# Attention round 0: stacks fetched in the projection stage, ten maxima units beside it, round 1's units inside round 0

## The chip, the cores and the metric

The kernel runs on one core of a Trainium2 chip. The metric is the device time of one execution in microseconds: the median over several runs. One more execution is recorded by the hardware profiler; all durations below are read from it.

## The reference

Two transformer layers over 4 sequences of 1024 tokens with 256 channels, all in fp32. Layer 0 has a random-feature attention (with rotary embedding) and a mixture of 8 experts, top 2. Layer 1, around which the change lies, has causal softmax attention with 16 heads of 16 channels, and a mixture of 16 experts, top 4, with a shared expert:

```python
def _L1_attn_ref(X, Wq, bq, Wk, bk, Wv, bv, Wo, bo):
    scale = 1.0 / sqrt(sqrt(d_head))
    Q = (X @ Wq.T + bq).reshape(B, S, H, d_head) * scale
    K = (X @ Wk.T + bk).reshape(B, S, H, d_head) * scale
    V = (X @ Wv.T + bv).reshape(B, S, H, d_head)
    scores = einsum('bhqd,bhkd->bhqk', Q, K)
    scores = where(causal, scores, -inf)
    out = einsum('bhqk,bkhd->bqhd', softmax(scores), V).reshape(B, S, D)
    return out @ Wo.T + bo
```

Each layer adds attention output times silu(mixture output) to its input; a layer norm stands before each.

## The kernel before

The program is a row of phases with a barrier of all engines between them: the first attention, experts of layer 0, the projection stage of layer 1 (`gate_and_project`), the causal attention, experts of layer 1, the shared expert and the gate. Each engine (TensorE or PE, VectorE or DVE, ScalarE or ACT, GpSimd or POOL, SyncE or SP with its DMA queue) has its own program, executed in the order in which it is written; semaphores join them. There is no planner: order is written out by hand with a helper `steps`, which for n = 0, 1, ... calls each stage with its own lag, stage(n - lag).

**First attention.** POOL's `rotate` (L701) multiplies q and k by cosine and sine into rot_a and rot_b, each with two buffers, and adds them.

**Projection stage** (L1132). 32 tiles of 128 tokens. Per step POOL gathers two expert rows per token (`rows`, lag 0) and multiplies (`product`, lag 2); ScalarE and VectorE combine, gate and add the residual. With lag 8 VectorE normalises a tile and TensorE transposes it (L1294); ScalarE keeps it and its high half; VectorE takes the low half (`low_half`, lag 9, L1222). With lag 9 TensorE computes V and router logits in three fp32r passes, with lag 13 one of four query/key tiles of a chunk of 512 tokens (`features`, six matmuls of 512 columns into one of four PSUM banks psK). ScalarE takes the high half of that (lag 13), VectorE the low half (lag 14, L1237), and SyncE stores both (256 KB each, L1338), beside V (L1329), the residual (L1319) and the transposed tile. The buffers of stored query/key and V tiles are four deep. The last features come in step 44, the last store in step 45. The order in which VectorE does its stages in a step n is: inverse root (n-5), normalise (n-8), low half (n-9), combine (n-1), V (n-10), residual (n-3), query/key low half (n-14). After the last step SyncE fetches the stacks of attention round 0 with `load_stacks` (L1602: four DMAs of 512 KB, L1607 and L1609), without waiting for them to land, and waits for all stores.

**Causal attention** (L1612). 16 rounds; round n does 4 heads of one sequence. A round works on a slot of three: the query stack QS and the key stack KS (high and low halves stacked on 126 partitions), two more rows for the negative row maxima (QS) and for ones (KS), and the values VA. Before the scores of a round the row maxima of all queries are needed. They are found in 38 units (`unit`): a unit is one to four matmuls into one PSUM bank psM of three (L1903) and one reduction by VectorE, with the causal mask added (L1799, on the diagonal) or plain (L1803). The units are in order of the query tile qt: unit 0 has four heads of 128 keys, units 1 and 2 two heads of 256, units 3 to 6 one head of 384, units 7 to 10 one head of 512, and so on. `whole` joins the maxima, TensorE turns them (L1913), VectorE's `negate` makes m_hi and m_lo (L1818 to L1822), and SyncE's `maxima_rows` stores them, waits, and loads them as two rows of QS.

The round itself has 12 steps of four score tiles (TensorE, L1920), each followed by ScalarE's exponential (L1883), POOL's cut on the diagonal (L1776), and with a lag of two steps the values (TensorE, L1932). Between the score tiles of round n TensorE does units: in steps 0 to 6 units 16 to 37 of round n+1, in steps 7 to 11 units 0 to 15 of round n+2 (`ahead`). VectorE does its share of them in the same order, with one piece of the router's work in each step (`route`).

The front of the phase, before round 0: VectorE does the first ten pieces of routing (L275 to L298), then the 38 units of round 0, `whole`, `negate`, and units 0 to 15 of round 1. TensorE waits for slot 0's stacks and VA, does the units of round 0, waits for slot 1, does units 0 to 15 of round 1, and begins with the scores. SyncE loads VA 0, ones, the stacks of round 1 (after POOL has zeroed slot 1), ones, and then does `maxima_rows(0, 0)`; the stacks of round n+2 are pulled at the start of round n. POOL zeroes QS and KS of slots 1 and 2 and makes the mask (`masks`, L2095).

## Time and profile before

| | us |
|---|---|
| median of 3 runs | 1855.63 (1853.65 to 1856.06) |
| the profiled execution | 1856.16 |
| its span, first to last instruction | 1854.4 |
| busy: PE, DVE, ACT, POOL | 1612.0, 1370.4, 1033.8, 672.0 |
| mean granted TensorE clock | 0.938 of full |
| projection stage | 555 to 716 |
| causal attention | 716 to 1278 |

A row of a timeline gives the start in us from the span's start, the duration, engine and line, the instruction with the tiles it writes and reads, and, in brackets, idle time of the engine before it and what ended it. A row of the windows gives busy us (and number of instructions) of PE, PE's weight loads, DVE, ACT and POOL in a stretch, then the granted TensorE clock (1.00 is 2.4 GHz, 0.50 is 1.2 GHz), the share in which the DMA engines were busy, and GB/s. Of operations that follow without a gap, the pace is the distance of their starts; the durations of matmuls overlap.

### The profile page before, as it was taken

How to read it: one execution, taken by the hardware profiler on the slowest of the kernel's cores; microseconds unless marked ns; L12 is line 12 of the kernel's file. 1: busy time of each engine (PE TensorE's matmuls, PEld its weight loads, DVE VectorE, ACT ScalarE, POOL GpSimd, SP SyncE). 2: the span in 40 equal slices, each digit the busy share in tenths (PEclk: the TensorE clock that was granted, in tenths of full speed). 3: DMA queues.
4: the chain of work that ended last, by engine and by line, in shares of the span. 5: the costliest groups of instructions: out<-in, count | busy, mean ns of one | idle time of the engine just before them, and what ended most of it. 6: DMA issues, size and time to landing. Idle time of an engine off the chain costs nothing. (4 is left out here: it accounts for less than half of the span.)

```text
span 1854.4 us, 34559 instructions
## 1 busy us (share of the span) xinstructions
PE 1612.0 (87%) x9650; PEld 1249.2 (67%) x9650; DVE 1370.4 (74%) x3710; ACT 1033.8 (56%) x2457; POOL 672.0 (36%) x842
## 2 busy tenths in 40 slices
PE   6897787679982776999999999997899999988997
PEld 5786676569982564555455555543799999967775
DVE  6778999356667876999888888852676666657777
ACT  2554565246654762466667676765556666643443
POOL 2545588510007643021136767630000000056662
PEclk9898899889995996799999999998999999989999
DMA  9322357654434888243244645404874444355552
GB/s 344 123 69 68 94 130 187 169 166 132 133 112 133 277 294 243 55 100 76 61 118 133 172 141 168 145 29 135 262 228 133 133 132 133 119 159 168 166 166 77
DMA packets 279591, 272.72 MB, mean 147 GB/s; under 512 B 121769, under 2 KB 248426, under 8 KB 277356
## 3 DMA queue, kind: packets, MB, share of 16 engines
q1 hardware_dynamic: 255672, 215.41, 39.6%
q0 software_dynamic: 18432, 50.36, 8.9%
q10 hardware_dynamic: 5332, 4.96, 0.8%
q8 instruction: 88, 1.44, 0.3%
q14 instruction: 67, 0.55, 0.1%
HBM read 136.84 MB, written 133.69 MB: 146 GB/s over the span
## 5 line engine op out<-in xcount | busy, mean ns | idle before, releaser
L1883 ACT ACTIVATE ca_PT<-ca_psS 128x512 f32<-128x512 f32 (+3 forms) x768 | 336.4, 494 | 204.0 <-PE ca_psS L1920 199.2
L1423 POOL DMA_INDIRECT g_y<-ys_scratch,pos x128 | 125.0, 977 | 425.7 <-POOLq L73 354.2
L1799 DVE CUSTOM_DVE_ANT_0 ca_masked_row<-ca_psM,mask_row 128x384 f32<-128x384 f32 (+3 forms) x512 | 224.2, 486 | 45.0 <-PE ca_psM L1903 42.9
L1803 DVE TENSOR_REDUCE ca_part<-ca_psM 128x1 f32<-128x512 f32 x256 | 163.5, 684 | 16.8 <-PE ca_psM L1903 15.4
L1920 PE MATMUL ca_psS<-ca_QS,ca_KS 128*128 128x512 f32 (+1 forms) x480 | 174.6, 367 | 1.4 <-ACT ca_PT L1883 1.4
L1932 PE MATMUL ca_psO<-ca_PT,ca_VA 128*17 128x512 f32 (+3 forms) x1536 | 161.0, 491 | 6.0 <-ACT ca_OT L1875 6.0
L1903 PE MATMUL ca_psM<-ca_KS,ca_QS 126*128 126x512 f32 (+2 forms) x480 | 159.5, 380 | 6.5 <-DVE ca_part L1799 4.2
L790 PE MATMUL fa_psO<-fa_weighed,ident 128*128 128x256 f32 x512 | 131.8, 416 | 38.1 <-DVE fa_weighed L585 38.1
L1920 PEld LDWEIGHTS ca_psS<-ca_QS,ca_KS 128*128 128x128 f32 x480 | 90.2, 189 | 86.8 <-ACT ca_PT L1883 58.1
L790 PEld LDWEIGHTS fa_psO<-fa_weighed,ident 128*128 128x128 f32 x512 | 104.6, 210 | 60.0 <-DVE fa_weighed L585 44.4
L391 POOL DMA_INDIRECT xs_scratch<-x_sb,pos x128 | 124.6, 973 | 55.9 <-ACT ca_PT L1883 34.1
L997 PE MATMUL f_psU<-ffn_lo,f_x_hi 128*128 x428 | 139.0, 325 | 0.0
L1086 DVE TENSOR_TENSOR f_x_lo<-f_psT,f_x_hi 128x256 fp32r<-128x256 f32 x214 | 90.7, 424 | 45.8 <-ACT f_x_hi L1038 45.6
L1044 ACT ACTIVATE f_silu<-f_psU 128x176 f32<-128x176 f32 x214 | 68.1, 318 | 100.1 <-PE f_psU L997 100.1
L1018 PE MATMUL f_psY<-ffn_lo,f_h_hi 128*128 x428 | 120.1, 281 | 0.0
L1774 POOL TENSOR_TENSOR ca_waited<-ca_waited 1x1 f32<-1x1 f32 x128 | 25.6, 200 | 259.9 <-ACT ca_PT L1883 258.6
L1903 PE MATMUL ca_psM<-spare 126*128 126x512 f32 (+3 forms) x288 | 98.3, 405 | 17.1 <-DMA ca_VA<-v_scratch 16.3
L1903 PEld LDWEIGHTS ca_psM<-ca_KS,ca_QS 126*128 126x128 f32 x480 | 88.8, 196 | 36.0 <-DVE ca_part L1799 17.4
L1094 DVE TENSOR_TENSOR f_h<-f_silu,f_psU 128x96 f32<-128x96 f32 x214 | 54.3, 254 | 76.7 <-ACT f_silu L1044 76.3
L1920 PE MATMUL ca_psS<-spare 128*128 128x512 f32 (+3 forms) x288 | 104.1, 375 | 2.7 <-ACT ca_PT L1883 2.5
L997 PE MATMUL f_psU<-ffn_hi,f_x_hi 128*128 x286 | 104.6, 366 | 0.0
L391 POOL DMA_INDIRECT xs_scratch<-s,pos x64 | 84.3, 1317 | 38.9 <-PE f_psT L967 24.2
(271 smaller groups left out, 4649.5 us busy)
## 6 DMA issues: line engine op xcount, KB each, us to landing
xs_scratch<-fa_blank SPq DMA_DIRECT2D x32, 640.0 KB, 4.9
x_sb<-xs_scratch SPq DMA_DIRECT2D x143, 128.0 KB, 2.1
ys_scratch<-x_sb SPq DMA_DIRECT2D x143, 128.0 KB, 1.7
xs_scratch<-fa_blank SPq DMA_DIRECT2D x32, 384.0 KB, 6.7
spare<-qk_scratch SPq DMA_DIRECT2D x24, 512.0 KB
ca_QS<-qk_scratch SPq DMA_DIRECT2D x20, 512.0 KB, 6.2
ca_KS<-qk_scratch SPq DMA_DIRECT2D x20, 512.0 KB, 7.5
x_sb<-in_ffn SPq DMA_DIRECT2D x16, 608.0 KB, 4.1
```

Source lines behind the costliest of these rows:

```text
L391: pool.indirect_dma_start(xs_dram, bass.IndirectOffsetOnAxis(pos[:, t, k:k + 1], 0), rows[:, t, :], None).then_inc(sent[i], 16)
L790: ins = pe.matmul(psO[i % 2][:, 0:NQ], ident[:], weighed[:, i % 2, g, :], start=g == 0, stop=g == KV_HEADS - 1)
L997: ins = pe.matmul(psU[i % 2][:, 0:WU], x[:, i % 2, k * P:(k + 1) * P], w[:, bass.ds(e, 1), k * WU:(k + 1) * WU].rearrange("p a n -> p (a n)"),
L1018: ins = pe.matmul(psY[i % 2][:, 0:HID], x, w[:, bass.ds(e, 1), first:first + HID].rearrange("p a n -> p (a n)"), start=start, stop=first = ...
L1086: dve.tensor_tensor(x_lo[:, i % 2, :], psT[i % 2][:, 0:HID], x_hi[:, i % 2, :].bitcast(F32), ALU.subtract)\
L1423: pool.indirect_dma_start(y[:, t % R, k, :], None, y_dram, bass.IndirectOffsetOnAxis(pos[:, t, k:k + 1], 0)).then_inc(got[t % R], 16)
L1799: ins = dve.tensor_tensor_reduce(masked_row[:, (n * NU + u) % BANKS, h * w:(h + 1) * w], bank[:, h * w:(h + 1) * w], mask_row[:, CHUNK - w ...
L1803: dve.tensor_reduce(part[:, k0 // CHUNK, h0:h0 + nh, qt], bank[:, 0:nh * w].rearrange("p (h k) -> p h k", h=nh), AX.X, ALU.max).then_inc(u ...
L1883: act.activation(PT[:, s % PTS, h, off:CHUNK], psS[(GH * s + h) % BANKS][:, off:CHUNK], ACT.Exp)\
L1903: ins = pe.matmul(bank[:, h * w:(h + 1) * w], QS[slot][0:STACK, h0 + h, qt * P:(qt + 1) * P], KS[slot][0:STACK, h0 + h, k0:k0 + w], start= ...
L1920: pe.matmul(psS[tile % BANKS][:, off:CHUNK], KS[slot][:, h, kt * P:(kt + 1) * P], QS[slot][:, h, c * CHUNK + off:(c + 1) * CHUNK], start=T ...
L1932: ins = pe.matmul(psO[STRIP * h:STRIP * h + VW, off:CHUNK], VA[:, slot, kt, VW * h:VW * (h + 1)], PT[:, s % PTS, h, off:CHUNK], start=kt = ...
```

## The change

It has six parts.

1. In the first attention rot_a and rot_b have one buffer each; POOL waits for its own add of the tile before (`rot_done`) before it overwrites them.
2. In the projection stage psK has three banks instead of four, and the bank that is freed, psM, takes maxima units. The mask is made by POOL at the start of this stage, ahead of the gathers, and lies, with the maxima `part`, in memory that the attention keeps.
3. SyncE fetches the stacks of round 0 at the end of step 32 of this stage, between the stores.
4. Units 0 to 9 of round 0 are done in steps 36 to 45, one at the end of each step, by TensorE and by VectorE.
5. In the attention VectorE begins with units 10 to 37 of round 0, `whole` and `negate`; the first ten pieces of routing come behind them. VA 0 and the pull of round 1's stacks come behind `maxima_rows(0, 0)` on SyncE. KS of slot 1 is zeroed by ScalarE, QS of slot 1 by POOL.
6. All 38 units of round 1 are done within round 0, in steps 2 to 6 (7 or 8 in each), followed as before by units 0 to 15 of round 2 in steps 7 to 11. TensorE waits for slot 1's stacks at the start of step 2. The later rounds keep their order.

```diff
@@ -702,7 +703,9 @@
...
-                q3, a3, b3 = (x[:, i % 2, :].rearrange("p (h d) -> p h d", d=D) for x in (qk, rot_a, rot_b))
+                if t >= 1:
+                    pool.wait_ge(rot_done, t)
+                q3, a3, b3 = (x.rearrange("p (h d) -> p h d", d=D) for x in (qk[:, i % 2, :], rot_a[:, :], rot_b[:, :]))
@@ -1129,14 +1132,26 @@
...
+EARLY_UNITS = 10
+MAXIMA_UNITS = [(qt, k0, w, h0, min(CHUNK // w, GH)) for qt in range(POS_TILES)
+                for k0, w in [(k, min(CHUNK, (qt + 1) * P - k)) for k in range(0, (qt + 1) * P, CHUNK)]
+                for h0 in range(0, GH, min(CHUNK // w, GH))]
...
+    BUFS, RING, KEPT, KBANKS = 4, 3, 8, 3
...
+    FETCH, LAST = TILES, TILES + BASE + QK_LAG
+    assert FETCH > BASE + QK_LAG + SPAN * QK_TILES
+
+    def unit_of(n):
+        u = n - (LAST + 1 - EARLY_UNITS)
+        return u if 0 <= u < EARLY_UNITS else None
@@ -1152,7 +1167,9 @@
...
-        psT, psV, psK = ps("psT", [P, HID], 2), ps("psV", [P, CHUNK], 2), ps("psK", [P, CHUNK], BUFS)
+        psT, psV, psK = ps("psT", [P, HID], 2), ps("psV", [P, CHUNK], 2), ps("psK", [P, CHUNK], KBANKS)
+        psM, = ps("psM", [P, CHUNK], 1)
@@ -1177,6 +1196,11 @@
...
+            pool.memset(mask_row[:, :], 0.0).then_inc(mask_blank, 1)
+            pool.wait_ge(mask_blank, 1)
+            diagonal = mask_row[:, CHUNK - P:CHUNK]
+            pool.affine_select(out=diagonal, in_=diagonal, compare_op=ALU.is_ge, fill=NEG, base=0,
+                               pattern=[[-1, P]], channel_multiplier=1).then_inc(mask_done, 1)
@@ -1234,11 +1258,28 @@
...
+            def unit(u):
+                qt, k0, w, h0, nh = MAXIMA_UNITS[u]
+                dve.wait_ge(unit_done, u + 1)
+                if k0 + w == (qt + 1) * P:
+                    for h in range(nh):
+                        ins = dve.tensor_tensor_reduce(masked_row[:, h * w:(h + 1) * w], psM[:, h * w:(h + 1) * w], mask_row[:, CHUNK - w:CHUNK],
+                                                       1.0, NEG, ALU.add, ALU.max, part[:, k0 // CHUNK, h0 + h, qt:qt + 1])
+                else:
+                    ins = dve.tensor_reduce(part[:, k0 // CHUNK, h0:h0 + nh, qt], psM[:, 0:nh * w].rearrange("p (h k) -> p h k", h=nh), AX.X,
+                                            ALU.max)
+                ins.then_inc(unit_out, 1)
...
+            def unit_beside(n):
+                if unit_of(n) == 0:
+                    dve.wait_ge(mask_done, 1)
+                if unit_of(n) is not None:
+                    unit(unit_of(n))
...
-            steps((5, inverse_root), (BASE, normalise), (BASE + 1, low_half), (1, combine), (BASE + 2, values), (3, residual),
-                  (BASE + QK_LAG + 1, qk_low_half))
+            steps((5, inverse_root), (BASE, normalise), (BASE + 1, low_half), (1, combine), (BASE + 2, values),
+                  (3, residual), (BASE + QK_LAG + 1, qk_low_half), (None, unit_beside))
@@ -1305,12 +1346,27 @@
...
-                if k >= BUFS:
-                    pe.wait_ge(qklo_out, k - (BUFS - 1))
-                three_passes(pe, psK[m][:], lambda j: w_qk[0][:, j, m * P:(m + 1) * P],
+                if k >= KBANKS:
+                    pe.wait_ge(qklo_out, k - (KBANKS - 1))
+                three_passes(pe, psK[k % KBANKS][:], lambda j: w_qk[0][:, j, m * P:(m + 1) * P],
...
-            steps((BASE, transpose), (BASE + 1, values_and_logits), (BASE + QK_LAG, features))
+            def unit(u):
+                qt, k0, w, h0, nh = MAXIMA_UNITS[u]
+                if u == 0:
+                    pe.wait_ge(first_in, 16 * (LOADS - 1))
+                else:
+                    pe.wait_ge(unit_out, u)
+                for h in range(nh):
+                    ins = pe.matmul(psM[:, h * w:(h + 1) * w], first_slot[0][0:STACK, h0 + h, qt * P:(qt + 1) * P],
+                                    first_slot[1][0:STACK, h0 + h, k0:k0 + w], start=True, stop=True, skip_group_check=True)
+                ins.then_inc(unit_done, 1)
+
+            def unit_beside(n):
+                if unit_of(n) is not None:
+                    unit(unit_of(n))
+            steps((BASE, transpose), (BASE + 1, values_and_logits), (BASE + QK_LAG, features), (None, unit_beside))
+            unit_beside(LAST)
@@ -1336,12 +1392,13 @@
...
-            steps((3, keep), (BASE + 2, save), (BASE + 2, store_v), (BASE + QK_LAG + 1, store_qk))
-            sp.wait_ge(zeroed, 2)
-            for m in range(QK_TILES):
-                sp.wait_ge(qk_stored[m], 32 * SPAN)
-                sp.wait_ge(v_stored[m], 16 * POS_TILES // BUFS)
-            load_stacks(sp, qk_dram, 0, first_slot[0], first_slot[1], first_in)
+            def fetch(n):
+                if n == FETCH:
+                    sp.wait_ge(zeroed, 2)
+                    for m in range(QK_TILES):
+                        sp.wait_ge(qk_stored[m], 32 * SPAN)
+                    load_stacks(sp, qk_dram, 0, first_slot[0], first_slot[1], first_in)
+            steps((3, keep), (BASE + 2, save), (BASE + 2, store_v), (BASE + QK_LAG + 1, store_qk), (None, fetch))
@@ -1643,15 +1698,20 @@
...
-        WHOLE, FIRST = 7, NU * 7 // 16
+        WHOLE, FIRST, FIRST_STEP = 7, NU * 7 // 16, 2
...
+        ahead_first = [list(range(NU * max(s - FIRST_STEP, 0) // (WHOLE - FIRST_STEP), NU * max(s + 1 - FIRST_STEP, 0) // (WHOLE - FIRST_STEP)))
+                       for s in range(WHOLE)] + ahead[WHOLE:]
+
+        def units_ahead(n, s):
+            later = n + 1 + s // WHOLE
+            return [(later, u) for u in (ahead if n else ahead_first)[s]] if later < ROUNDS else []
@@ -1731,17 +1789,19 @@
...
-            for n in range(SLOTS):
-                if n:
-                    sp.wait_ge(zeros_done, 2 * n)
-                if 1 <= n < SLOTS - 1:
-                    pull(n)
-                if n == 0:
-                    pull_values(n)
-                    sp.wait_ge(filled, 1)
+            def one_key_rows(n):
                 sp.dma_start(KS[n][STACK:P, :, :].rearrange("r h (c n) -> r (h c) n", n=P).bitcast(F32),
-                             one_rows[:, :].unsqueeze(1).broadcast_to([2, GH * POS_TILES, P])).then_inc(ones_done, 16)
+                             one_rows[:, :].unsqueeze(1).broadcast_to([2, GH * POS_TILES, P])).then_inc(ones_done[n], 16)
+            sp.wait_ge(filled, 1)
+            one_key_rows(0)
             maxima_rows(0, 0)
+            pull_values(0)
+            sp.wait_ge(zeros_done, 1)
+            sp.wait_ge(keys_zeroed, 1)
+            pull(1)
+            one_key_rows(1)
+            sp.wait_ge(zeros_done, 3)
+            one_key_rows(2)
@@ -1852,15 +1913,12 @@
...
             dve.memset(psO[:, :], 0.0).then_inc(blank_done, 1)
-            for at in range(FRONT):
-                route(at)
-            dve.wait_ge(masked, 1)
-            for u in range(NU):
+            for u in range(EARLY_UNITS, NU):
                 unit(0, u)
             whole(0)
             negate(0)
-            for u in range(FIRST):
-                unit(1, u)
+            for at in range(FRONT):
+                route(at)
             for n in range(ROUNDS):
                 for s in range(NS):
                     step(n, s)
@@ -1966,18 +2027,18 @@
...
-            pe.wait_ge(stack_in[0], 16 * LOADS)
-            for u in range(NU):
+            for u in range(EARLY_UNITS, NU):
                 unit(0, u)
             transpose_maxima(0)
-            pe.wait_ge(stack_in[1], 16 * LOADS)
-            for u in range(FIRST):
-                unit(1, u)
-            pe.wait_ge(ones_done, 16 * SLOTS)
             pe.wait_ge(blank_done, 1)
             for n in range(ROUNDS):
                 pe.wait_ge(m_in[n % SLOTS], (n // SLOTS + 1) * 16)
+                if n < SLOTS:
+                    pe.wait_ge(ones_done[n], 16)
                 for s in range(NS):
+                    if n == 0 and s == FIRST_STEP:
+                        pe.wait_ge(stack_in[0], 16 * LOADS)
+                        pe.wait_ge(stack_in[1], 16 * LOADS)
                     if s == WHOLE and n + 2 < ROUNDS:
                         pe.wait_ge(stack_in[(n + 2) % SLOTS], ((n + 2) // SLOTS + 1) * (16 * LOADS))
                     step(n, s)
...
```

## Rows read from the trace of the kernel before

**Rows 1.** Windows, round 1: length, busy us per engine, clock, DMA share.

```profile
789.00:806.00 17.00, 16.16 (x102) 8.51 (x102) 16.58 (x45) 9.72 (x26) 5.23 (x12) 1.00 0.67 149
```

**Rows 2.** Timeline of VectorE, attention's front: start us, duration us, line, instruction.

```profile
716.67 0.63 DVE L275 TENSOR_REDUCE r_top<-logits 128x32 f32<-128x512 f32 x1
...
724.35 0.69 DVE L298 TENSOR_TENSOR r_same<-r_one,r_rank 128x512 f32<-128x512 f32 x1
...
726.88 0.29 DVE L1799 CUSTOM_DVE_ANT_0 ca_masked_row<-ca_psM,mask_row 128x128 f32<-128x128 f32 x1 [1.83 <-PE ca_psM L1903]
...
727.73 0.42 DVE L1799 CUSTOM_DVE_ANT_0 ca_masked_row<-ca_psM,mask_row 128x256 f32<-128x256 f32 x1
...
729.10 0.55 DVE L1799 CUSTOM_DVE_ANT_0 ca_masked_row<-ca_psM,mask_row 128x384 f32<-128x384 f32 x1
...
732.87 0.69 DVE L1799 CUSTOM_DVE_ANT_0 ca_masked_row<-ca_psM,mask_row 128x512 f32<-128x512 f32 x1
...
751.17 0.28 DVE L1822 TENSOR_TENSOR ca_m_lo<-ca_m_f,ca_m_hi 32x128 fp32r<-32x128 f32 x1
...
761.46 0.69 DVE L1803 TENSOR_REDUCE ca_part<-ca_psM 128x1 f32<-128x512 f32 x1
...
795.57 0.69 DVE L1803 TENSOR_REDUCE ca_part<-ca_psM 128x1 f32<-128x512 f32 x1
```

**Rows 3.** Timeline of TensorE, first maxima, scores of round 0, scores of round 1.

```profile
725.58 2.07 PE L1903 MATMUL ca_psM<-spare 126*128 126x128 f32 x8 [16.28 <-DMA ca_VA<-v_scratch]
...
760.26 0.73 PE L1920 MATMUL ca_psS<-spare 128*128 128x512 f32 x1
...
794.31 0.50 PE L1920 MATMUL ca_psS<-ca_QS,ca_KS 128*128 128x512 f32 x1
```

**Rows 4.** Timeline of SyncE's queue: last store, the next phase's first, a pull.

```profile
711.20 0.46 SPq L1338 DMA_DIRECT2D qk_scratch<-gp_qk_lo  x1
...
716.10 0.39 SPq L1704 DMA_DIRECT2D ca_VA<-v_scratch  x1
...
753.65 0.57 SPq L1607 DMA_DIRECT2D ca_QS<-qk_scratch  x1
```

**Rows 5.** Timeline of TensorE in the projection stage, two of them after a wait.

```profile
696.43 0.39 PE L121 MATMUL gp_psK<-gp_XT_hi,wqk_lo 128*128 128x512 f32 x1
...
696.67 0.38 PE L1294 MATMUL gp_psT<-ident,x_sb 128*128 128x128 f32 x2
...
683.13 0.44 PE L1294 MATMUL gp_psT<-ident,x_sb 128*128 128x128 f32 x2 [1.29 <-DVE x_sb L1217]
...
620.73 0.69 PE L1294 MATMUL gp_psT<-ident,x_sb 128*128 128x128 f32 x2 [2.33 <-DVE x_sb L1217]
```

**Rows 6.** Timeline of VectorE in the projection stage: normalise, then low half.

```profile
695.87 0.40 DVE L1217 TENSOR_SCALAR x_sb<-x_sb,mean_rstd 128x256 f32<-128x256 f32 x1
...
696.19 0.42 DVE L1222 TENSOR_TENSOR gp_XT_lo<-gp_psT,gp_XT_hi 128x256 fp32r<-128x256 f32 x1
```

**Rows 7.** Timeline of TensorE: units of four and of two heads at full clock.

```profile
813.74 0.56 PE L1903 MATMUL ca_psM<-spare 126*128 126x128 f32 x4
...
814.43 0.41 PE L1903 MATMUL ca_psM<-spare 126*128 126x256 f32 x2
```

**Rows 8.** Timeline of POOL: first product of the projection stage, and the mask's select.

```profile
565.36 0.72 POOL L1188 TENSOR_TENSOR s<-s,gp_c 128x256 f32<-128x256 f32 x1 [1.18 <-ACT gp_c L1253]
...
724.41 0.78 POOL L2109 TENSOR_SCALAR_AFFINE_SELECT mask_row<-mask_row 128x128 f32<-128x128 f32 x1 [0.23 <-POOL mask_row L2106]
```

**Rows 9.** Windows, the pull of round 2's stacks.

```profile
755.00:765.00 10.00, 10.00 (x28) 6.86 (x28) 9.30 (x29) 3.21 (x7) 0.66 (x2) 0.56 1.00 238
```

**Rows 10.** Windows: the projection's end, its last wait, the first maxima.

```profile
684.00:712.00 28.00, 24.99 (x130) 19.90 (x129) 18.60 (x42) 14.88 (x36) 0.68 (x1) 1.00 0.92 348
...
712.00:716.00 4.00, 0.00 (x0) 0.00 (x0) 0.00 (x0) 0.00 (x0) 0.00 (x0) 0.58 1.06 319
...
726.00:746.00 20.00, 19.72 (x44) 11.26 (x43) 19.11 (x70) 0.00 (x0) 6.14 (x2) 0.50 0.47 110
```

More of the change, by code:

```diff
@@ L1167, in steps @@
         def steps(*stages):
-            for n in range(TILES + max(lag for lag, _ in stages)):
+            for n in range(TILES + max(lag for lag, _ in stages if lag is not None)):
                 for lag, stage in stages:
-                    if lag <= n < TILES + lag:
+                    if lag is None:
+                        stage(n)
+                    elif lag <= n < TILES + lag:
                         stage(n - lag)
@@ L1634, in causal_attention @@
         PT = sb("PT", [P, PTS, GH, CHUNK])
-        units = [(qt, k0, w, h0, min(CHUNK // w, GH)) for qt in range(POS_TILES)
-                 for k0, w in [(k, min(CHUNK, (qt + 1) * P - k)) for k in range(0, (qt + 1) * P, CHUNK)]
-                 for h0 in range(0, GH, min(CHUNK // w, GH))]
+        units = MAXIMA_UNITS
         NU = len(units)
@@ L1837, in step @@
             def step(n, s):
-                todo = [(n + 1 + s // WHOLE, u) for u in ahead[s] if n + 1 + s // WHOLE < ROUNDS]
+                todo = units_ahead(n, s)
                 for k in todo[:1]:
@@ L1949, in step @@
             def step(n, s):
-                todo = [(n + 1 + s // WHOLE, u) for u in ahead[s] if n + 1 + s // WHOLE < ROUNDS]
+                todo = units_ahead(n, s)
                 for h in range(GH):
```

63 lines of the change are left out of this document (27 added, 36 removed).

## The prediction

> **What bounds the kernel now.** I read the slices of the page first, then the windows, then the timelines of the stretch that the diff touches: the end of the projection stage (to 716), the front of the attention (716 to 760) and round 0 (760 to 794). The chain that ended last lies in the final stage and says nothing here. All stages are separated by barriers, so what the touched stretch gains or loses before round 1 is carried to the end unchanged.
>
> In the rounds the reader is to see VectorE busy 16.6 us of 17, at full TensorE clock [rows 1]. TensorE shows as busy too, but its ends are modelled; VectorE's row has hardly a hole. The 38 maxima units of a round are most of its work, so early rounds go at VectorE's pace.
>
> At the front VectorE runs routing pieces from 716.67 (to 725.04, 8.4 us), waits for the stacks until 726.88, does the 38 units of round 0, ends m_lo at 751.45, does 16 units of round 1 until 761.46, and reaches the same place of the next round (unit 16 of round 2) at 795.57 [rows 2]. TensorE starts at 725.58, its first scores come at 760.26, round 1's at 794.31 [rows 3]. As VectorE sets that pace, the ruler is its own time: from the start s = 716.1 of the phase [rows 4] to 795.57 are 79.5 us.
>
> **The projection stage: what is added.** Units 0 to 9 are done in steps 36 to 45, at the end of TensorE's step and of VectorE's step. VectorE executes in order: its unit waits for TensorE's unit matmul of the same step, and the normalise of the next step is queued behind it; TensorE's next transposes wait for that normalise. Before, TensorE went from the last feature matmul (696.43) to the transposes (696.67) without a pause [rows 5], since the normalise had begun at 695.87 [rows 6]. Now each step has a chain in place of those 0.24 us:
> - Step 36 to 37: unit 0's four matmuls end 0.56 after they start [rows 7]; VectorE needs 0.9 for the unit (units 0 to 2 take 2.22 together, the first 0.85 [rows 2]); normalise 0.40 [rows 6]; 0.1 for two hand-overs; and 0.2 because the values now wait for the low half, which ends 0.34 after the normalise [rows 6]. Together 2.15.
> - Steps 37 to 39: units 1 and 2 take 0.41 on TensorE [rows 7] and 0.7 on VectorE: 1.85 each.
> - Step 39 to 40: no transposes are left, but the values wait for the last low half (0.42 [rows 6]) behind unit 3: 0.35 + 0.5 + 0.42 + 0.1 = 1.4.
> That is 7.2 us. In steps 40 to 44 nothing on TensorE waits for VectorE's latest step; five units add their matmuls, about 0.2 each: 1.0. VectorE's unit 8 pushes the last low half by 0.2. Loads landing late for unit 0: the transposes of step 33 are at 683.13 and those of step 38 at 696.67 [rows 5], so step 32 ends near 683.5 and step 36 near 694.3; a pull without its V takes some 10 us (below). I take 0.3, bounds 0 and 2. This term is hidden by nothing else.
>
> The three instead of four psK banks: features of tile k wait for the low half of k-3, which VectorE did two steps earlier; nothing. The mask on POOL ahead of the gathers costs about 1.5 us (its select alone 0.78 after 0.23 of waiting), of which 1.18 fall into the idle time before the first product [rows 8]: 0.3, bounds 0 and 1.5. The rotation buffers of the first attention: POOL executes its own instructions in order, so the added wait is only on its own last add; nothing, at most 32 times 0.05.
>
> SyncE: four load issues (about 0.6 each) leave the end of the stage, where the next phase began 4.4 us after the last store was issued (711.66 to 716.10) [rows 4]. What remains is that store's landing and the barrier. Bounds 0 and -2.5; I take -1.3. Moved into step 32, they push the stores of steps 33 to 35 by 2 us on SyncE; stores are needed back four steps later, and TensorE is now slower there, so I count nothing.
>
> Sum at the start of the attention: 7.2 + 1.0 + 0.2 + 0.3 + 0.3 - 1.3 = **+7.7 us**.
>
> **The front of the attention, from its start s.** VectorE's first unit follows TensorE's first matmul by 1.3 [rows 2, 3]; stacks and routing no longer stand before it: s+1.3. The 28 units left, the whole maxima and m_lo took 732.87 to 751.45, 18.6 [rows 2]: s+19.9. Then SyncE stores the maxima and sends their rows. In the kernel before, m_lo ended at 751.45 and the next pull started at 753.65 [rows 2, 4]: 2.2 later. **Round 1's stacks are now pulled only here**, behind the maxima rows on the same queue. The pull of 753.65 kept the DMA engines fully busy from 755 to 765 [rows 9], 11.3 after its start, and V of round 0 now goes before it (another 1.8: 0.6 to issue it and 1.2 of transfer, its 0.27 of the pull's 2.3 MB by those ten us). So TensorE passes the wait of step 2 at s+19.9+2.2+11.3+1.8 = s+35.2. The scores of steps 0 and 1 start early (2.2 after m_lo plus some 2 for the maxima rows to land, my estimate, so s+24) but end long before. VectorE does its routing meanwhile and two more pieces (some 9 us, to s+29) and then idles for about 8. Its first unit of round 1 comes at s+36.8 (TensorE is at 1.2 GHz by then: scores, weights, matmuls of unit 0 take about 1.6). Then units 0 to 15, 10.0 (751.45 to 761.46), and all that before lay between 761.46 and 795.57, 34.1, less the two pieces done (1.4): s+79.5. Before: s+79.5. The six us of ten units and the nine of an earlier start are all lost in the wait for the stacks: **0 us**. Bounds: -8 if the stacks came at once, +3 if TensorE at half clock can't feed 7.6 units a step; the row of 753.65 fixes the transfer closely, so I keep 0, with -2 and +3 as its own range.
>
> ScalarE's zeroing of KS1 and POOL's of QS1 are done long before s+22. Zeroing of slot 2 stays before its pull. Later rounds keep their order.
>
> **One rule on the clock.** Rows first: TensorE was recorded busy 19.7 of 20 us in 726 to 746, and the granted clock stayed 0.50, that is 1.2 GHz [rows 10]. The Trainium skill, "TensorE: Matmul & The Clock Gate", Part 1 on the HAM clock gate, says that the throttled state is the default and that sustained activity releases it. By the row the clock comes back late in step 2 or later, as in the sum; by the page, earlier, and the sum would be about 1 us lower. The measurement decides.
>
> **Sum.** 1856.2 (the profiled execution; span 1854.4) + 7.7 + 0 = 1863.9. The median of the runs is 0.5 lower, so I forecast **1863.5**.
>
> **Rivals.**
> - *The early scores carry through (faster).* If TensorE and ScalarE, not VectorE, set the pace of round 0, its twelve steps took 34.05 (760.26 to 794.31 [rows 3]), ten of them 28.4; from step 2 at s+35.2, with s at 723.8, round 1 starts at 787.4 instead of 794.3: -6.9, **1848.8** beside the median. It decides if VectorE can take 16 more units (10 us) in those 28 us without lengthening them. Against it: VectorE is under 5% idle [rows 1]. For it: TensorE's rows look as full. 9%.
> - *No lockstep (no change).* If the normalise is not late, TensorE pays only its own matmuls, about 2.1 for the units: +2.1 + 0.3 - 1.3 = +1.1, **1856.8**. It needs VectorE to be ahead of TensorE's unit, which the order in the code denies; but a shorter gap and a quicker transfer together end there too. 13%.
> - *The stores queue behind the stacks (much slower).* Between 684 and 712 the DMA engines are busy 0.92 of the time [rows 10], which leaves some 4 us at the 1.06 seen when they are saturated; the four loads are 8.8 (ten less 1.2 for V [rows 9]). Then 4.9 more are paid at the end of the stage: +12.6, **1868.4**. Against it: TensorE's own delay of 8 us opens room. Of about the same size: the gaps of lockstep (1.3 to 2 us) halve the clock. One of 2.33 ended with two transposes at half speed (0.69 instead of 0.38 to 0.44), one of 1.29 did not [rows 5]. 18%. The Trainium skill, "DMA: Bandwidth & Descriptors", section "Queues, rings and completion order", says that on each DMA engine descriptors are consumed in ring order, which is what would put the later stores of SyncE's queue behind the loads; no row before shows loads ahead of stores.
> - *Forecast as above.* 60%.
>
> **Numbers.** A difference under 0.2%, 3.7 us, can't be told from no change. Faster: the first rival, 0.09. Same: the second, 0.13. Slower: 0.60 + 0.18 = 0.78. The bounds of the forecast itself (loads 0 to 2, barrier 0 to -2.5, lockstep 6 to 9, front -2 to +3) give 1860 to 1868; for eight in ten I go down to 1857.5, into the second rival, and up to 1870.
>
> **What would show it.** Right: on TensorE, gaps before the transposes of steps 37 to 39 ended by the normalise; attention's first unit on VectorE near 725, m_lo near 743.5; DMA busy until 759; VectorE idle from about 753 to 760, ended by TensorE's unit matmul; round 1's scores near 802. Wrong: no gaps in steps 37 to 39; stacks of round 1 landing before VectorE has ended its routing; or holes in VectorE's round 0 after step 2.

## The result, and the profile after

The changed kernel takes 1866.76 us (median of ten runs, 1853.18 to 1873.44), the kernel before, on the same chips, 1854.93 (ten runs, 1844.61 to 1862.07): ratio 1.0072, 95% interval [1.0048, 1.0095], so 13.4 us slower. The profiled execution took 1870.12, its span is 1868.0, 13.6 over the 1854.4 of before, with the same mean clock of 0.938.

First the windows of the changed kernel (length; busy time of PE, PEld, DVE, ACT, POOL; granted clock; DMA share; GB/s): the projection's end, then the first maxima, the wait for the stacks, and two stretches of round 0.

```profile
684.00:712.00 28.00, 21.49 (x106) 16.30 (x105) 16.44 (x51) 11.20 (x28) 0.00 (x0) 0.94 0.90 289
...
732.00:750.00 18.00, 10.34 (x20) 5.05 (x19) 16.51 (x46) 0.63 (x1) 4.23 (x2) 0.50 0.15 32
750.00:770.00 20.00, 12.97 (x40) 7.98 (x40) 8.60 (x32) 6.09 (x15) 2.29 (x6) 0.51 1.01 222
770.00:790.00 20.00, 16.79 (x66) 9.11 (x66) 17.61 (x50) 7.28 (x14) 0.77 (x2) 0.83 0.05 9
790.00:807.00 17.00, 16.34 (x97) 8.38 (x100) 16.09 (x56) 8.44 (x21) 3.29 (x8) 1.00 0.06 14
```

From 684 to 712 TensorE is busy 21.5 us, where it was 25.0 [rows 10], at nearly the same DMA share. From 750 to 770 VectorE, which sets the pace of the rounds [rows 1], is busy 8.6 us of 20.

The timeline of TensorE in the projection stage (start us, duration us, line, instruction, in brackets the idle time before it and what ended it): units 0 and 1, the steps behind them, unit 9, and the first matmul of the attention.

```profile
694.94 0.66 PE L1361 MATMUL gp_psM<-spare 126*128 126x128 f32 x4 [1.37 <-DMA spare<-qk_scratch]
697.07 0.44 PE L1335 MATMUL gp_psT<-ident,x_sb 128*128 128x128 f32 x2 [1.47 <-DVE x_sb L1241]
...
700.30 0.63 PE L121 MATMUL gp_psK<-gp_XT_lo,wqk_hi 128*128 128x512 f32 x1
700.73 0.63 PE L121 MATMUL gp_psK<-gp_XT_hi,wqk_lo 128*128 128x512 f32 x1
701.16 0.45 PE L1361 MATMUL gp_psM<-spare 126*128 126x256 f32 x2
702.80 0.44 PE L1335 MATMUL gp_psT<-ident,x_sb 128*128 128x128 f32 x2 [1.19 <-DVE x_sb L1241]
...
706.98 0.44 PE L1335 MATMUL gp_psT<-ident,x_sb 128*128 128x128 f32 x2 [1.20 <-DVE x_sb L1241]
...
710.90 0.39 PE L121 MATMUL gp_psV<-wvr_hi,gp_XT_hi 128*128 128x274 f32 x1 [0.99 <-DVE gp_XT_lo L1246]
...
719.25 0.40 PE L121 MATMUL gp_psK<-gp_XT_hi,wqk_lo 128*128 128x512 f32 x1
...
720.68 0.49 PE L1361 MATMUL gp_psM<-spare 126*128 126x512 f32 x1 [0.79 <-DVE part L1268]
725.16 2.35 PE L1964 MATMUL ca_psM<-spare 126*128 126x512 f32 x4 [3.99 <-PEq L73]
```

VectorE's timeline beside it: unit 0, and the normalise queued behind it.

```profile
695.75 0.29 DVE L1268 CUSTOM_DVE_ANT_0 wqkvr_raw<-gp_psM,mask_row 128x128 f32<-128x128 f32 x1 [3.68 <-PE gp_psM L1361]
...
696.60 0.41 DVE L1241 TENSOR_SCALAR x_sb<-x_sb,mean_rstd 128x256 f32<-128x256 f32 x1
696.93 0.42 DVE L1246 TENSOR_TENSOR gp_XT_lo<-gp_psT,gp_XT_hi 128x256 fp32r<-128x256 f32 x1
```

The chain of the prediction is there: unit on TensorE, unit on VectorE, normalise, transposes, three times over (waits of 1.47, 1.19 and 1.20). In the kernel before TensorE had gone from 696.43 to 696.67 without a pause [rows 5] and the normalise had been early [rows 6]. In step 40 the values wait 0.99 for the low half. Two things are there beside it: 1.37 of waiting for the stacks, and six feature matmuls 0.43 apart instead of 0.23, which is half clock (1.2 GHz).

The front of the attention: SyncE's queue, then TensorE, then VectorE.

```profile
721.68 0.43 SPq L1394 DMA_DIRECT2D qk_scratch<-gp_qk_lo  x1
725.34 0.80 SPq L1793 DMA_DIRECT2D spare<-ca_one_rows  x1
744.57 0.34 SPq L1777 DMA_DIRECT2D m_scratch<-ca_m_hi  x1
...
747.24 0.61 SPq L1664 DMA_DIRECT2D ca_QS<-qk_scratch  x1
```

```profile
750.04 4.00 PE L1981 MATMUL ca_psS<-spare 128*128 128x512 f32 x8 [6.38 <-issue]
...
760.41 0.55 PE L1981 MATMUL ca_psS<-spare 128*128 128x256 f32 x1 [6.37 <-DMA ca_VA<-v_scratch]
...
766.03 1.91 PE L1993 MATMUL ca_psO<-ca_PT,ca_VA 128*17 128x512 f32 x8
```

```profile
744.27 0.28 DVE L1883 TENSOR_TENSOR ca_m_lo<-ca_m_f,ca_m_hi 32x128 fp32r<-32x128 f32 x1
...
761.85 0.29 DVE L1860 CUSTOM_DVE_ANT_0 ca_masked_row<-ca_psM,mask_row 128x128 f32<-128x128 f32 x1 [9.13 <-PE ca_psM L1964]
...
768.92 0.69 DVE L1860 CUSTOM_DVE_ANT_0 ca_masked_row<-ca_psM,mask_row 128x512 f32<-128x512 f32 x1 [2.13 <-PE ca_psM L1964]
...
776.48 0.29 DVE L1860 CUSTOM_DVE_ANT_0 ca_masked_row<-ca_psM,mask_row 128x128 f32<-128x128 f32 x1 [1.91 <-PE ca_psM L1964]
```

Against [rows 4] the last store is issued 10.5 us later (721.68 for 711.20) and the attention starts 9 later (725.1 for 716.1). m_lo comes at 744.3 for 751.2 [rows 2]: the ten units and the routing are gone from before it. Then VectorE waits 9.13 us for TensorE's first unit of round 1, which waits for the stacks, and in round 0 twice more, 2.13 and 1.91, for unit matmuls at half clock. Before the first of the two TensorE is in eight value matmuls, which take 1.91 (the row of 766.03) and in the same round, at full clock, 1.05 (at 791.62).

### The profile page after: what moved, and what is told of

The parts are those of the page before. It is cut to its first block and busy times, and to the rows that moved or that the text cites. A ratio compares the mean times of both kernels' runs of the same rounds, so it can differ in the third digit from the quotient of the medians.

```text
span 1868.0 us, 34558 instructions
## 1 busy us (share of the span) xinstructions
PE 1612.4 (86%) x9650; PEld 1247.2 (67%) x9650; DVE 1375.4 (74%) x3710; ACT 1036.3 (55%) x2458; POOL 668.5 (36%) x841
## 5 line engine op out<-in xcount | busy, mean ns | idle before, releaser
L1860 DVE CUSTOM_DVE_ANT_0 ca_masked_row<-ca_psM,mask_row 128x512 f32<-128x512 f32 (+1 forms) x497 | 218.4, 487 | 56.7 <-PE ca_psM L1964 54.9
L1864 DVE TENSOR_REDUCE part<-ca_psM 128x1 f32<-128x512 f32 x256 | 163.3, 685 | 16.4 <-PE ca_psM L1964 14.6
L793 PE MATMUL fa_psO<-fa_weighed,ident 128*128 128x256 f32 x512 | 131.1, 414 | 38.7 <-DVE fa_weighed L586 38.7
L1000 PE MATMUL f_psU<-ffn_lo,f_x_hi 128*128 x428 | 138.7, 324 | 0.0
L1964 PEld LDWEIGHTS ca_psM<-ca_KS,ca_QS 126*128 126x128 f32 x480 | 88.8, 196 | 38.7 <-DVE part L1860 16.2
L1981 PEld LDWEIGHTS ca_psS<-spare 128*128 128x128 f32 x288 | 55.6, 197 | 71.8 <-ACT ca_PT L1941 39.6
```

The lines of the kernel that those rows point to most:

```text
L793: ins = pe.matmul(psO[i % 2][:, 0:NQ], ident[:], weighed[:, i % 2, g, :], start=g == 0, stop=g == KV_HEADS - 1)
L1000: ins = pe.matmul(psU[i % 2][:, 0:WU], x[:, i % 2, k * P:(k + 1) * P], w[:, bass.ds(e, 1), k * WU:(k + 1) * WU].rearrange("p a n -> p (a n)"),
L1860: ins = dve.tensor_tensor_reduce(masked_row[:, at % BANKS, h * w:(h + 1) * w], bank[:, h * w:(h + 1) * w], mask_row[:, CHUNK - w:CHUNK], 1 ...
L1864: dve.tensor_reduce(part[:, k0 // CHUNK, h0:h0 + nh, qt], bank[:, 0:nh * w].rearrange("p (h k) -> p h k", h=nh), AX.X, ALU.max).then_inc(u ...
L1964: ins = pe.matmul(bank[:, h * w:(h + 1) * w], QS[slot][0:STACK, h0 + h, qt * P:(qt + 1) * P], KS[slot][0:STACK, h0 + h, k0:k0 + w], start= ...
L1981: pe.matmul(psS[tile % BANKS][:, off:CHUNK], KS[slot][:, h, kt * P:(kt + 1) * P], QS[slot][:, h, c * CHUNK + off:(c + 1) * CHUNK], start=T ...
```

## The ruler for the experiments

Whole times of this kernel scatter by some 10 us to either side, and much of that lies before the projection stage (in the fourteen traces its first transposes start between 573.1 and 585.5 us). So each experiment is read at six points of its own timelines: A, the first transposes of the projection stage; B, those of step 33; C, the end of the last feature; s, the attention's first instruction; M, the end of m_lo; X, the first exponential of round 1. From X to the end all fourteen traces need 1059.1 to 1063.5 us. The last columns are the timed difference to the kernel before, (ratio - 1) times its median, with its interval.

| kernel | A-B | B-C | C-s | A-s | s-M | s-X | A-X | timed, us | interval |
|---|---|---|---|---|---|---|---|---|---|
| before | 99.8 | 26.2 | 6.8 | 132.7 | 35.4 | 78.8 | 211.5 | | |
| b_again | 99.2 | 26.2 | 6.8 | 132.2 | 35.1 | 78.5 | 210.7 | +0.6 | -3.5 to 4.6 |
| e7_rot_alone | 99.1 | 26.1 | 6.8 | 132.1 | 34.9 | 77.7 | 209.7 | +0.7 | -3.7 to 5.4 |
| changed | 100.5 | 37.4 | 5.5 | 143.4 | 19.4 | 83.0 | 226.4 | +13.4 | 8.9 to 17.6 |
| e9_changed_fetch_29 | 103.8 | 36.1 | 5.5 | 145.4 | 19.4 | 81.9 | 227.3 | +20.4 | 13.7 to 27.1 |
| e2_pull_first | 99.3 | 35.5 | 5.5 | 140.2 | 19.4 | 72.7 | 212.9 | +8.1 | 3.3 to 13.1 |
| e1_unit_behind | 99.5 | 31.2 | 7.5 | 138.2 | 19.4 | 80.6 | 218.8 | +17.8 | 10.7 to 24.8 |
| e3_both | 101.2 | 32.5 | 5.9 | 139.6 | 19.4 | 73.1 | 212.7 | +6.7 | 2.2 to 11.1 |
| e4_all_three | 100.6 | 30.2 | 7.6 | 138.3 | 19.4 | 69.4 | 207.8 | +1.9 | -2.4 to 5.9 |
| e8_fetch_29 | 103.5 | 28.0 | 5.5 | 136.9 | 19.4 | 69.4 | 206.3 | -1.7 | -6.1 to 2.8 |
| e11_all_again | 106.0 | 30.3 | 5.4 | 141.7 | 19.4 | 69.3 | 211.0 | -1.3 | -6.3 to 3.5 |
| e5_no_early | 99.9 | 32.5 | 6.4 | 138.8 | 25.7 | 90.9 | 229.7 | +18.3 | 12.0 to 24.8 |
| e6_fetch_alone | 100.7 | 32.7 | 6.5 | 139.9 | 33.8 | 77.0 | 216.9 | +5.7 | 1.1 to 10.2 |
| e10_before_fetch_29 | 105.1 | 27.4 | 6.4 | 138.9 | 33.8 | 77.2 | 216.1 | +4.1 | 0.0 to 8.2 |

These points have a scatter of their own. Up to s the changed kernel and e2 execute the same code, and A to s is 143.4 and 140.2; so do e8 and e11, with 136.9 and 141.7. The three kernels that fetch at the end agree better, 132.1 to 132.7. A difference of 3 us in the stage between two single traces of the others is therefore no finding.

## Experiments

**e1: VectorE's units one step later.**

```diff
...
-                  (3, residual), (BASE + QK_LAG + 1, qk_low_half), (None, unit_beside))
+                  (None, unit_behind), (3, residual), (BASE + QK_LAG + 1, qk_low_half))
+            unit_behind(LAST + 1)
```
Step n now executes the unit of step n-1, behind the values.

> The changed kernel with one thing different: VectorE executes each of the ten early units one step later, behind the normalise, the low half and the values of that step, so nothing that TensorE needs next is queued behind a unit. Theory (lockstep): the gaps of 1.47, 1.19 and 1.20 us before the transposes of steps 37 to 39 and of 0.99 before the values go, and with them the half clock of step 37; the attention starts 6 to 8 us earlier than the 725.1 of the changed kernel (717 to 719), the front after it is as long as there, total 1861 instead of 1868. Rival (loads and stores contend, or TensorE's unit matmuls are dear in themselves): the start moves by less than 2 us, total 1866 to 1868. If the first unit's wait of 1.37 for its stacks stays, that part is the load's own.

Only part of it came. B to s is 38.7 us instead of 42.9. The first transposes behind unit 0 and those of the third step wait no more. Unit 0 still waits 0.80 for its stacks, and one wait of 1.25 before transposes is left. TensorE, and then VectorE, which shows where the second is from:

```profile
684.72 0.66 PE L1362 MATMUL gp_psM<-spare 126*128 126x128 f32 x4 [0.80 <-DMA spare<-qk_scratch]
...
689.72 0.44 PE L1336 MATMUL gp_psT<-ident,x_sb 128*128 128x128 f32 x2 [1.25 <-DVE x_sb L1241]
```

```profile
686.66 0.42 DVE L1253 TENSOR_TENSOR gp_v_st<-gp_psV,bias_v 128x256 f32<-128x256 f32 x1 [3.58 <-DMA v_scratch<-gp_v_st]
```

V's buffer is refilled four tiles later, and its store has not landed. So behind the lockstep stood a second wait, for stores, that the trace of the changed kernel does not show. By the six points this kernel is 7.5 us faster than the changed one (5.2 in the stage, 2.4 in the front, which the edit does not touch); its timed ratio, 1.0096 [1.0058, 1.0134] from six runs, doesn't show that, and between the two I can't decide for the whole program.

**e2: round 1's stacks pulled first.**

```diff
             one_key_rows(0)
-            maxima_rows(0, 0)
             pull_values(0)
...
             pull(1)
             one_key_rows(1)
+            maxima_rows(0, 0)
```

> The changed kernel with one thing different: SyncE issues V of round 0 and the stacks of round 1 at the start of the attention, as soon as slot 1 is zeroed, and the maxima rows behind them. Theory (the wait for the stacks costs the front): the pull runs from 3.6 us after the start to about 15, m_lo at 19.4 is not touched, TensorE goes through steps 0 and 1 without a stop, round 1's first unit reaches VectorE at about 30 us after the start instead of 36.7, round 1's scores come 5 to 7 us earlier; total 1862. Rival (TensorE at half clock sets the pace of round 0): VectorE's two holes of 2.13 and 1.91 grow to 8 or more together and the total moves by less than 2 us, 1866 to 1868.

The front shrinks by 10.3 (s to X 72.7 for 83.0), more than the 5 to 7 expected. TensorE and VectorE of this kernel:

```profile
748.78 0.95 PE L1964 MATMUL ca_psM<-ca_KS,ca_QS 126*128 126x128 f32 x4
...
751.08 0.34 PE L1964 MATMUL ca_psM<-ca_KS,ca_QS 126*128 126x384 f32 x1
```

```profile
749.87 0.29 DVE L1860 CUSTOM_DVE_ANT_0 ca_masked_row<-ca_psM,mask_row 128x128 f32<-128x128 f32 x1 [1.78 <-PE ca_psM L1964]
...
755.44 0.69 DVE L1860 CUSTOM_DVE_ANT_0 ca_masked_row<-ca_psM,mask_row 128x512 f32<-128x512 f32 x1 [0.63 <-PE ca_psM L1964]
```

The first unit is on VectorE 29.4 us after s (720.5) and not 36.7: 7.3 is the wait for the stacks. The other 3 are the two holes of 2.13 and 1.91, which are 0.63 and less here. Windows of this kernel and, below, of the changed one show the clock beside it:

```profile
741.00:751.00 10.00, 6.36 (x20) 4.87 (x21) 7.25 (x19) 5.28 (x12) 1.80 (x4) 0.50 0.75 184
751.00:761.00 10.00, 7.66 (x37) 3.32 (x36) 9.30 (x30) 1.61 (x6) 1.58 (x4) 1.00 0.33 63
761.00:771.00 10.00, 7.89 (x40) 4.45 (x42) 9.53 (x32) 4.24 (x8) 0.00 (x0) 1.00 0.00 0
```

```profile
760.00:765.00 5.00, 3.98 (x15) 3.21 (x15) 3.12 (x18) 1.54 (x4) 0.77 (x2) 0.50 0.99 195
765.00:770.00 5.00, 5.00 (x18) 2.51 (x18) 2.87 (x11) 0.83 (x3) 0.00 (x0) 0.55 0.97 217
770.00:773.00 3.00, 1.93 (x5) 0.72 (x4) 2.96 (x9) 0.28 (x1) 0.77 (x2) 0.99 0.31 62
773.00:777.00 4.00, 4.00 (x17) 2.12 (x18) 2.09 (x8) 0.80 (x2) 0.00 (x0) 0.58 0.00 0
```

Without the pause TensorE goes on from the scores into the units and has full clock at 751. With a pause of 6.37 it stays at 1.2 GHz until about 770, shows 2.4 for three microseconds and falls to 1.2 once more; each hole of VectorE lies in or just behind such a stretch. The rival, that half clock would eat the gain, is refuted.

**e3: both edits.**

> Both edits in one kernel: VectorE's early units one step later, and the stacks of round 1 pulled at the start of the attention. If the two costs are independent, the gains add: 12 to 13 us off the changed kernel, total 1855 to 1856, the same as the kernel before. If one clock state feeds both, the sum is more than the parts; if TensorE sets the pace of round 0, it is 1861.

Stage and front are those of e1 and e2: A to s 139.6, s to X 73.1. The total of the expectation came, 13.7 us off the changed kernel from A to X, but not by adding: e2 alone has 13.5 of it (A to X 212.9 for 212.7 here), and e1 alone had 7.5. With the pull first, taking the lockstep away shows 0.6 us from A to s, within the scatter, since V waits 3.32 us for its store here too. From B to C it is 3.0 (35.5 to 32.5). The timed ratio is 1.0036 [1.0012, 1.006], e2's 1.0044 [1.0018, 1.0071]: no difference between them either. What is left is in the stage, 7 us longer than before's.

**e4: and round 1's first 16 units in front of round 0.**

```diff
...
+            for u in range(FIRST):
+                unit(1, u)
             for at in range(FRONT):
                 route(at)
...
```
That is VectorE's part, beside the edits of e1 and e2; TensorE likewise, behind a wait for slot 1; the table ahead_first goes.

> As the kernel with both edits, and round 1's first 16 units again in front of round 0 (before VectorE's routing pieces), as in the kernel before, the other 22 in its first seven steps. Theory: the attention's start is 1 to 2 us later than the 716.1 of the kernel before; m_lo at 19.4 after the start, 16 units in 10, 8.4 of routing, so that VectorE stands at 38 us after the start where the kernel before stood at 45.4, without a wait; then 34.1 as there. Total 1856.2 + 1.5 - 7 = 1850 to 1851, faster than both kernels. Rival (TensorE at half clock, 38 units at the front and early scores behind it, sets the pace): 1855 or more.

The front is 9.1 us shorter than that of b_again (69.4 for 78.5), 2 more than expected. The stage is 6 longer, where 1 to 2 were expected. Timed 1.001 [0.9987, 1.0032]: no difference.

**e5: no early units, all else as changed** (`EARLY_UNITS = 0`).

> The changed kernel with none of the maxima units in the projection stage (all 38 at the front of the attention), the stacks still fetched at step 32, round 1's stacks still pulled behind the maxima rows. Counted from the transposes of step 33. Theory (the ten units cost the stage, the order of the pulls costs the front): the attention starts 31.7 us after them (33.0 in the kernel before, 42.9 in the changed one); the front is 6 us longer than in the changed kernel, since the wait for the stacks only moves behind m_lo; round 1's first exponential at 120 to 121 (111.8 before, 125.9 changed), total 1863. Rival (fetching at step 32 is what costs the stage): the attention starts at 38 or later.

Here the rival won, in the part that I had expected least. B to s is 38.9 and not 31.7, with not one unit in the stage. The front is 7.9 longer than the changed kernel's (90.9 for 83.0), where 6 were expected.

**e6: the fetch at step 32, in the kernel before.**

```diff
...
-            steps((3, keep), (BASE + 2, save), (BASE + 2, store_v), (BASE + QK_LAG + 1, store_qk))
-            sp.wait_ge(zeroed, 2)
...
-            load_stacks(sp, qk_dram, 0, first_slot[0], first_slot[1], first_in)
+            def fetch(n):
+                if n == TILES:
+                    sp.wait_ge(zeroed, 2)
...
+                    load_stacks(sp, qk_dram, 0, first_slot[0], first_slot[1], first_in)
+            steps((3, keep), (BASE + 2, save), (BASE + 2, store_v), (BASE + QK_LAG + 1, store_qk), (None, fetch))
```

> The kernel before with one thing different: the stacks of round 0 are fetched at step 32 of the projection stage and not at its end. Theory (loads among the stores cost nothing): the attention starts 31.5 to 32.5 us after the transposes of step 33 instead of 33.0, VectorE's wait of 1.84 for the stacks behind its routing goes, round 1's first exponential comes 2 to 4 us sooner than the 111.8 of the kernel before, total 1852. Rival (the stores queue behind the stacks): features or values wait for their stores, the stage is 2 to 5 us longer, total 1856 to 1860.

The rival again: the stage is 7.5 us longer, the front 1.5 shorter, the kernel slower at 1.0031 [1.0006, 1.0055]. VectorE, TensorE, and a window of this kernel with, behind it, the same window of the kernel before:

```profile
697.92 0.42 DVE L1231 TENSOR_TENSOR gp_v_st<-gp_psV,bias_v 128x256 f32<-128x256 f32 x1 [3.97 <-DMA v_scratch<-gp_v_st]
```

```profile
701.02 0.69 PE L1296 MATMUL gp_psT<-ident,x_sb 128*128 128x128 f32 x2 [3.86 <-DVE x_sb L1219]
701.36 0.59 PE L121 MATMUL gp_psV<-wvr_hi,gp_XT_hi 128*128 128x274 f32 x1
```

```profile
696.00:704.00 8.00, 4.14 (x16) 3.33 (x16) 3.90 (x9) 2.93 (x8) 0.00 (x0) 0.73 1.06 400
```

```profile
696.00:704.00 8.00, 8.00 (x46) 6.90 (x45) 5.23 (x12) 3.92 (x11) 0.00 (x0) 1.00 0.78 292
```

V's buffer waits for its store behind the loads, the normalise stands behind V on VectorE, TensorE stops 3.86 us and goes on at half clock (transposes 0.69, as in the row of 620.73 [rows 5]). The DMA engines are busy 1.06, the share that the prediction took for saturated, where the same window of the kernel before has 0.78.

**e7: the rotation buffers alone** (rot_a and rot_b single, with GpSimd's wait, in the kernel before).

> The kernel before with one thing different: rot_a and rot_b of the first attention have one buffer each, with GpSimd's wait for its own add. The prediction took this for nothing: GpSimd waits 123 us for ScalarE in that stage anyway; ratio 1.000, total within 3 us of the kernel before. Rival: the timed medians of the four kernels run so far lie some 4 to 5 us above what their traces give from step 33 on, and this edit is the part that lies before it; then the ratio is 1.002 to 1.003.

1.0004 [0.998, 1.0029], and B to X 110.6: nothing, as predicted.

**e8: as e4, the stacks fetched at step 29** (`FETCH = TILES - 3`).

> The kernel of all three edits (units one step behind on VectorE, the pull first, round 1's first 16 units in front), with the stacks of round 0 fetched at step 29 instead of 32. Theory (the wait of unit 0 is the load's own time): unit 0 starts without the wait of 0.8 to 1.4 us and the stage is 1 to 2 us shorter; round 1's first exponential 105.5 to 106.5 us after the transposes of step 33 (107.2 with the fetch at 32), total 1849 to 1850. Rival: the loads collide with the stores of steps 29 to 33 and the gain is lost, 107 or more.

Counted from B as the expectation has it, 102.8 instead of 107.2, better than hoped. But B is itself late: A to B went from 100.6 to 103.5. From A only 1.5 is left of the gain over e4, and e11 below does not repeat it.

**e9: the changed kernel with the fetch at 29.**

> The changed kernel with one thing different: the stacks of round 0 are fetched at step 29 instead of 32; VectorE's units stay in lockstep with TensorE's. Counted from the transposes of step 33. Theory (lockstep and the late landing of the V stores are two causes that overlap in the changed kernel): no wait for the stacks, no half clock in step 37, the gaps before the transposes of steps 37 to 39 stay; the last feature ends at 34 to 35 (26.2 in the kernel before, 28.0 without lockstep and with the fetch at 29, 37.4 in the changed kernel). Rival (the contention was the whole of it): 28 to 30.

B to C is 36.1: the gaps of lockstep stay (1.47, 1.20, 1.20 and 0.99), the wait for the stacks is gone. The contention only moved ahead of B. ScalarE of this kernel, and its window:

```profile
673.80 0.51 ACT L1290 ACTIVATE gp_c<-gp_y,wts 128x256 f32<-128x256 f32 x1 [6.48 <-DMA gp_y<-ys_scratch,pos]
```

```profile
664.00:674.00 10.00, 5.11 (x27) 3.74 (x26) 3.46 (x9) 3.46 (x9) 0.74 (x1) 1.00 0.99 258
```

At step 29 it is GpSimd's gathers that land late: TensorE's transposes at 677.20 wait 6.99 for what follows from them. ScalarE's last two waits for gathered rows are 0.29 and 6.48 here, 4.85 and 1.82 in e8, 5.29 and 2.89 in e10; in the kernel before the last but one tile waits 1.93 and the last not at all.

**e10: the kernel before with the fetch at 29.**

> The kernel before with one thing different: the stacks of round 0 are fetched at step 29 of the projection stage. With the fetch at step 32 alone VectorE's V of step 36 waited 3.97 us for the store of its buffer, the next transposes 3.86, and the last feature ended at 32.7 after the transposes of step 33 instead of 26.2. Theory (it is the place: at 29 the V buffers' stores land in time, since the stage still has waits of its own there): last feature at 26 to 27, round 1's first exponential at 109 to 110 (111.8 before), total 2 us below the kernel before. Rival (a fetch anywhere costs the stage): 30 or more.

From B it looks almost harmless (C at 27.4, expected 26 to 27; X at 111.1, expected 109 to 110); from A the stage is 6.4 longer, as with 32. Timed 1.0022 [1.0, 1.0044], at the edge of no difference. The rival "a fetch anywhere costs the stage" is right; my ruler started too late for it.

**b_again and e11: once more before, once more e8.**

> The kernel before once more, unchanged: a second profile of it, to see how far its own points move from one execution to the next. Both theories: ratio 1.000 within its interval; from the transposes of step 33 to round 1's first exponential 110.5 to 113 (111.8 in the first profile); what differs by more lies before the projection stage.

> The kernel of all three edits with the fetch at step 29, once more. By its trace it is 8.9 us ahead of the kernel before at round 1's first exponential, by its timed runs 0.9991 [0.9967, 1.0015]. If the trace is right, this second set lies at 0.995 to 0.997; if the timed runs are, at 0.999 to 1.001.

The kernel before repeats its points: B to X 111.5 for 111.8. e11 doesn't repeat e8: its stage is 141.7 for 136.9, with waits of 4.26 and 4.31 for gathered rows on ScalarE where e8 had 4.85 and 1.82. The timed ratios agree with each other, 0.9991 [0.9967, 1.0015] and 0.9993 [0.9966, 1.0019]: the best version is no different from the kernel before. Of the two readings in the expectation the timed runs were right, and by e11's own trace A to X is 211.0, within the 209.7 to 211.5 of the kernels before.

## Why the prediction was right, and where it was not

The forecast was 1863.5, the median is 1866.8. Direction, range, and most of the events were right. The sum was 6 us short (7.7 for 13.6 by the spans), in two terms: the stage, A to s, is 10.7 us longer where 7.7 were forecast, and the front, s to X, 4.2 where 0 was; A itself lies 1.6 earlier in this trace. The median is nearer to the third rival's 1868.4 than to the forecast, and that rival's mechanism is the one that e6 shows. That the total still fell into the range is in part luck: 0.3 stood for the loads, which cost 6.9 by themselves. With 6.9 in its place the stage's sum would be 14.3, and 10.7 were measured only because the two waits overlap.

**The lockstep (predicted 7.2 to step 40).** Right in the changed kernel's own trace: the gaps are 1.47, 1.19, 1.20 and 0.99, 4.85 together, and the matmuls of units 0 to 3 take 0.66, 0.45, 0.40 and 0.34, another 1.85: 6.7. The five units in the tail cost about 0.2 each (TensorE's units are 1.57 apart, the features were 1.39). With the 1.37 for the stacks and the 1.5 at half clock (below) that is 10.5 of the 11.2 by which B to C is longer than before. Taking the lockstep away pays less where V's stores are late. A to s is 143.0 on average in the three kernels with it (changed, e2, e9) and 138.9 in the five with the units behind (e1, e3, e4, e8, e11): 4.1. By the place of the fetch it is 3.1 at step 32 (141.8 for 138.7) and 6.1 at step 29 (145.4 for 139.3), from one to three traces each, with the scatter said above. From B to C, which leaves out the late gathers, step 29 has 36.1 with lockstep (e9) and 28.0 and 30.3 without (e8, e11): 5.8 to 8.1, around the 7.2 of the prediction. At step 32 V's wait for its store (3.58, 3.32 and 2.38 in e1, e3 and e4) takes part of it back.

**Loads and stores ("I take 0.3, bounds 0 and 2", "so I count nothing").** This is the step that failed by most. The three kernels that fetch within the stage and have no units (e5, e6, e10) need 139.2 from A to s, against 132.3 for before, b_again and e7: 6.9 us for the fetch alone, at step 32 or at 29. e5 has the mask and the three psK banks, e6 and e10 have not, and they lie within 1.1 of each other: these two cost nothing that shows. With ten units and no lockstep it is 138.9: done one step later, the units cost nothing that shows either. The prediction had this mechanism as its third rival, worked out at 4.9 us of DMA time without slack, and gave it 18%; what it took for an argument against ("TensorE's own delay of 8 us opens room") describes the changed kernel: during the pauses of lockstep the V stores land, V never waits for one, and only 1.37 shows as the price of the loads. Beside it is a stretch at half clock, some 1.5 (six feature matmuls longer by 0.2, three of V by 0.1), which e2, with the same code in the stage and a wait of 0.95 for the stacks, does not have. Two causes that overlap: with both 10.7, with the fetch alone 6.9, and neither can be read off the other's gaps. The Trainium skill, "DMA: Bandwidth & Descriptors", section "Queues, rings and completion order", says that each DMA engine consumes descriptors in ring order; e6 agrees: the store of V issued at 687.91, behind the four loads issued from 684.12 to 686.60, is what V waits for, 3.97 us. It doesn't prove the order, since a store would also be late behind DMA engines that are merely full.

**SyncE's four issues (predicted -1.3).** C to s fell from 6.80 to 5.47: -1.3.

**Mask and rotation buffers.** A to B 100.5 for 99.2 to 99.8, e7 at 1.0004: within 1 us, as predicted.

**The front (predicted 0, own range -2 to +3).** Point by point it stands: m_lo at s+19.4 (19.9), TensorE through the wait at s+35.3 (35.2), VectorE's first unit at s+36.7 (36.8), idle before it 9.1 (8). Then the forecast leaves the trace: round 1's scores start at 807.5, forecast near 802, and s to X is 83.0 for 78.8, 4.2 more. That is the two holes of 2.13 and 1.91, and "holes in VectorE's round 0 after step 2" was the prediction's own sign of being wrong. The prediction had TensorE at half clock feeding 7.6 units a step as its bound of +3 and set it to 0, because VectorE's row is full at full clock [rows 1]. That step of the prediction failed. In the kernel before the granted clock was back at 1.00 from 764, 4 us after the first scores of round 0 (760.26), so the round ran at full clock. Here it is back at about 770, twenty after the first scores, with the pause of 6.37 in between, which the change itself makes. In e2, which has no such pause, it is back 6 us after the first scores and the holes are 0.63 and 0.40.

**The rule on the clock.** The prediction expected the clock back late in step 2 or later by the row [rows 10]; 0.50 in 732 to 750 and until about 770 bears that out. By the rule of the Trainium skill, "TensorE: Matmul & The Clock Gate", Part 1 on the HAM clock gate, which has sustained activity release the throttled state, it took the clock to be back earlier, with 1 us less, and that did not come. The trace is no test of the rule, since TensorE pauses 6.38 before the scores and 6.37 behind them.

**The rivals.** "Early scores carry through" failed on the wait for the stacks. With it gone (e2) the front is 5.8 shorter than b_again's, where this rival needed 14.6 (its 6.9 and the stage's 7.7): VectorE is busy 9.53 of 10 us in a window of round 0, so the 16 units more are paid there. "No lockstep" is e1 in the trace: not 1.1 but 5.9 over before, since the stores take its place.

What stays open: the timed differences of e1 to e4 lie 5 to 6 us (e1: 10) above what A to X gives against the 210.6 of the three kernels before, the others within 4, and nothing in the traces outside A to X accounts for it. All four were timed on one chip against the same 29 runs of the kernel before, and none of the others was, so an offset of that one comparison can't be told from an effect of the edits.

## What to carry to other kernels

Here 2.1 MB of loads, moved into a stage whose DMA engines were busy 0.92 of the time, cost 6.9 us at either of the two places tried, where the forecast had 0.3; look for slack in the DMA row before looking for an idle engine. A unit of work that two engines do in the same step of their programs ties them; one step later on the second engine it cost nothing that showed. And price a wait by an experiment that takes it out: what its gaps hide behind them is not in the trace. Start the ruler ahead of the first thing that the change can touch: with B as its start, the fetch at step 29 looked almost free.

## What the runs showed of the hardware

Before and after its pause of 6.37 us the changed kernel's TensorE was at 1.2 GHz; then the granted clock came back to 2.4 GHz for three microseconds and fell again (0.99 in 770 to 773, 0.58 in 773 to 777), with TensorE recorded busy 1.93 of the three and all of the four. Pauses of 1.37 and 1.47 around unit 0 were followed by half clock in step 37 of the changed kernel; pauses of 0.95 and 1.47 at the same place in e2, and of 1.47 in e9, were not. After 3.86 in e6 it was half clock too (0.50 from 701 to 706). In e2, which pauses 5.60 before the scores, the clock was at full level by 751, 6 us after they began; in the changed kernel it took until about 770, ten after the pause of 6.37 and twenty after the scores.
